# Last layer of a four-layer pair network: the order of TensorE's products and transposes, the way the totals are made, and the place of the residual copies

## The reference, cut to what matters

```python
x = x + _L3_conv_ref(_gn(x), L3_conv_Ws, L3_conv_Wm, L3_conv_bm)

# in _L3_conv_ref(X, Ws, Wm, bm), with L(v, i) = v @ Ws[i - 1]:
ret = L(X, 10) + L(X.transpose(0, 2, 1, 3), 11)
ret = ret + (L(sum_of_rows, 6) + L(sum_of_cols, 8) + L(diag_part, 12))[:, :, None, :]
ret = ret + (L(sum_of_rows, 7) + L(sum_of_cols, 9) + L(diag_part, 13))[:, None, :, :]
ret = ret + 2.0 * L(sum_diag_part, 14)[:, None, None, :]
diag_term = L(diag_part, 1) + L(sum_of_rows, 3) + L(sum_of_cols, 4) + (L(sum_diag_part, 2) + L(sum_all, 5))[:, None, :]
ret = ret + diag_term[:, :, None, :] * eye[None, :, :, None]
return jax.nn.relu(ret @ Wm + bm)
```

## Time and profile before

| | before |
|---|---|
| median of 3 runs | 1118.38 us (1118.35 to 1118.80) |
| the profiled execution | 1116.33 us, of which its span (first to last instruction) is 1114.5 us |
| busy over the span | PE 1029.5 us (92%), DVE 743.7, ACT 519.3, POOL 410.6 |
| granted TensorE clock, mean | 0.958 of full |
| last norm block, from the barrier to the next one | 1062.9 to 1066.9 us |
| block of `layer3` | 1066.9 to 1114.5 us, 47.6 us |
| PE busy in one pair of its steps | 3.11 of 4.40 us |

### The profile page before, as it was taken

How to read it: one execution, slowest core, us unless ns; L and a number is a source line. 1 busy time by engine, 2 the same in 40 slices (tenths; PEclk the granted TensorE clock), 3 DMA queues, 4 the chain that set the end, 5 groups by cost and what they waited for, 6 DMA issues and landing times. The chain is left out here.

```text
span 1114.5 us, 24968 instructions
## 1 busy us (share of the span) xinstructions
PE 1029.5 (92%) x9092; PEld 736.1 (66%) x9092; DVE 743.7 (67%) x3631; ACT 519.3 (47%) x1133; POOL 410.6 (37%) x555
## 2 busy tenths in 40 slices
PE   5887999999999699779999999999999999999966
PEld 4435888888887343357777777777777777777632
DVE  3685888888887323456767777676777667676353
ACT  2485777777777100124343443434344343434344
POOL 0154666666666200011332323233232333323245
PEclk8899999999999699859999999999999999999969
DMA  8000000000000000000000000000000000000033
GB/s 174 2 0 2 3 2 3 3 3 2 3 2 3 1 1 1 10 1 1 1 2 1 2 1 2 1 1 1 1 1 2 1 1 1 2 1 1 1 86 141
DMA packets 14045, 13.01 MB, mean 12 GB/s; under 512 B 3300, under 2 KB 11748, under 8 KB 13924
## 3 DMA queue, kind: packets, MB, share of 16 engines
q1 hardware_dynamic: 12548, 10.84, 3.9%
q10 hardware_dynamic: 1376, 0.59, 0.3%
HBM read 5.14 MB, written 4.19 MB: 8 GB/s over the span
## 5 line engine op out<-in xcount | busy, mean ns | idle before, releaser
L1606 PE MATMUL quad<-theta,nat 128*128 128x512 f32 x512 | 240.8, 593 | 0.0
L730 POOL TENSOR_TENSOR nat<-nat,arena 128x512 f32<-128x512 f32 x128 | 131.7, 1050 | 39.4 <-DVE arena L788 35.6
L1614 PEld LDWEIGHTS quad<-flat 128*128 128x128 f32 x768 | 104.3, 190 | 46.9 <-ACT flat L1400 24.1
L1606 PEld LDWEIGHTS quad<-theta,nat 128*128 128x128 f32 x512 | 87.5, 191 | 61.7 <-issue 61.7
L1614 PE MATMUL quad<-flat 128*128 128x128 f32 x768 | 124.7, 285 | 2.1 <-ACT flat L1400 1.0
L788 DVE CUSTOM_DVE_ANT_0 nat<-quad,arena 128x128 f32<-128x128 f32 x512 | 111.2, 282 | 1.4 <-PE quad L874 1.4
L1400 ACT ACTIVATE flat<-quad 128x256 f32<-128x256 f32 x192 | 73.5, 383 | 74.5 <-PE quad L1614 57.9
L747 ACT ACTIVATE nat<-bank 128x512 f32<-128x512 f32 x128 | 73.1, 598 | 65.3 <-PE bank L882 65.3
L1357 POOL COPY img<-flat 64x256 f32<-64x256 f32 x63 | 25.1, 399 | 186.2 <-DVE nat L1515 171.7
L882 PE MATMUL bank<-const,nat 128*128 128x128 f32 x512 | 73.3, 276 | 8.8 <-ACT nat L747 8.0
L752 ACT ACTIVATE nat<-nat 128x512 f32<-128x512 f32 x128 | 77.2, 634 | 3.8 <-POOL nat L730 3.8
(11 more groups left out here) (386 smaller groups left out, 2313.2 us busy)
## 6 DMA issues: line engine op xcount, KB each, us to landing
out<-nat SPq DMA_DIRECT2D x16, 256.0 KB, 2.0
flat<-img SPq DMA_DIRECT2D x2, 640.0 KB, 8.5
flat<-img SPq DMA_DIRECT2D x1, 512.0 KB, 4.9
const<-in_constants ACTq DMA_DIRECT2D x1, 400.5 KB, 3.2
flat<-img SPq DMA_DIRECT2D x1, 256.0 KB, 3.3
arena<-in_L_conv_Ws SPq DMA_DIRECT2D x1, 240.0 KB
nat<-in_x SPq DMA_DIRECT2D x4, 0.2 KB, 12.1
arena<-in_L_conv_Wq ACTq DMA_DIRECT2D x1, 32.0 KB, 7.0
```

Source lines behind the costliest of these rows:

```text
L730: pool.tensor_tensor(scored, scored, of_head(least[b], h).broadcast_to([128, ROWS, L]), ALU.subtract).then_inc(lowered, 1)
L1606: return pe.matmul(m.quad[:, n, :], vT[:, col(n)], m.theta[:, part, :], start=(part == 0), stop=False, skip_group_check=True)
L1614: last = pe.matmul(m.quad[:, row, place * C:(place + 2) * C], a8[g % 2][:, col(row)], zs[half][k % 2][:, n, :], start=False, stop=(k == 2) ...
```

## The change

Five edits, all in the last layer:

- On PE the two products of later steps stand ahead of the two transposes in each turn of the loop, where they stood behind them.
- Each total is made for both halves of the partitions: each weight is multiplied twice, once into each half, and the column and diagonal totals take only the 64 columns of that half (every second one, `own`). The constants are added by PE in the same accumulation, as products with a vector repeated over 64 columns (`level`).
- DVE copies the finished totals: one copy for `of_row` and one for `of_col` instead of six instructions, two for `diag_pair` instead of four.
- Five of the sixteen residual copies of ACT stand in the norm block, ahead of the square root.
- The other eleven stand ahead of the first Relu; none is among the steps any more.

```diff
@@ group_norm
+            if act_aside is not None:
+                act_aside(act)
             act.wait_ge(S("group_var"), layer + 1)
@@ layer3
-    totals, diag_totals = B[0], B[1]
+    row_totals, col_totals, diag_totals = B[0][:, 0:L], B[0][:, L:L + L // 2], B[1][:, 0:L // 2]
+    EARLY = 5
+    def first_copies(act):
+        for t in range(EARLY):
+            copy_half(act, t)
-    group_norm(nc, m, 3, pool_aside=sums_of_cols, dve_aside=raw_rows)
+    group_norm(nc, m, 3, pool_aside=sums_of_cols, dve_aside=raw_rows, act_aside=first_copies)
@@ DVE
             dve.wait_ge(terms_made, 1)
-            for q in range(2):
-                step(dve.tensor_copy(level[halves[q], 0:1], totals[halves[0], 2 * L:2 * L + 1]))
-                dve.tensor_scalar(of_col[halves[q], :], totals[halves[0], L + q:2 * L:2], level[halves[q], 0:1], None, ALU.add)
-                step(dve.tensor_copy(of_row[halves[q], :], totals[halves[0], 0:L]))
+            dve.tensor_copy(of_row, row_totals)
+            step(dve.tensor_copy(of_col, col_totals))
...
                 for q in range(2):
-                    step(dve.tensor_copy(level[halves[q], 1:2], diag_totals[halves[0], L:L + 1]))
-                    last = dve.tensor_scalar(diag_pair[halves[q], :, q], diag_totals[halves[0], q:L:2], level[halves[q], 1:2], None, ALU.add)
+                    last = dve.tensor_copy(diag_pair[halves[q], :, q], diag_totals[halves[q], :])
@@ ACT
-            AHEAD = 10
-            for t in range(AHEAD):
-                copy_half(t)
+            for t in range(EARLY, STEPS3):
+                copy_half(act, t)
...
-                if t + AHEAD < STEPS3:
-                    copy_half(t + AHEAD)
@@ PE
+            def total(into, vectors, first=True, done=True):
+                for n, (weights, vector_of) in enumerate(vectors):
+                    for q in range(2):
+                        last = pe.matmul(into[halves[q], :], weights, vector_of(q), start=(first and n == 0),
+                                         stop=(done and n == len(vectors) - 1), skip_group_check=True)
+                return last
...
+            def own(vector):
+                return lambda q: vector[:, q:L:2]
+            def level(vector):
+                return lambda q: vector.broadcast_to([vector.shape[0], L // 2])
...
             for t in range(0, STEPS3, 2):
-                turn(t)
-                turn(t + 1)
                 for later in (t + 4, t + 5):
                     if later < STEPS3:
                         mixed(later)
+                turn(t)
+                turn(t + 1)
```

More of the change, by code:

```diff
@@ L394, in _, with group_norm @@
             turn_banks(at_bank, BANKS)
-def group_norm(nc, m, layer, loads=(), loaded=None, pool_aside=None, dve_aside=None):
+def group_norm(nc, m, layer, loads=(), loaded=None, pool_aside=None, dve_aside=None, act_aside=None):
     rows = 128
@@ L1776, in layer3 @@
     col_half = m.take(L)
-    of_row, of_col, level = m.take(L), m.take(L // 2), m.take(2)
+    of_row, of_col = m.take(L), m.take(L // 2)
     diag_pair = m.take(L).rearrange("p (s q) -> p s q", q=2)
@@ L1816, in raw_rows, with copy_half @@
         dve.tensor_copy(diag_raw, m.img[0:C, 0:L * L:L + 1])
-    group_norm(nc, m, 3, pool_aside=sums_of_cols, dve_aside=raw_rows)
+    EARLY = 5
+    def copy_half(act, t):
+        act.activation(*residual_half(0, t, t + 1), ACT.Copy).then_inc(m.sem("copied"), 1)
+    def first_copies(act):
+        for t in range(EARLY):
+            copy_half(act, t)
+    group_norm(nc, m, 3, pool_aside=sums_of_cols, dve_aside=raw_rows, act_aside=first_copies)
     prepared, terms_made = S("prepared"), S("terms_made")
@@ L1908, in _, with whole @@
         def _(pe):
-            def total(bank, place, vectors):
-                for n, (weights, vector) in enumerate(vectors):
-                    last = pe.matmul(bank[halves[0], place], weights, vector, start=(n == 0), stop=(n == len(vectors) - 1))
-                return last
+            def total(into, vectors, first=True, done=True):
[3 more added lines that the diff above has]
+                                         stop=(done and n == len(vectors) - 1), skip_group_check=True)
+                return last
+            def whole(vector):
+                return lambda q: vector
+            def own(vector):
+                return lambda q: vector[:, q:L:2]
+            def level(vector):
+                return lambda q: vector.broadcast_to([vector.shape[0], L // 2])
             def mixed(t):
@@ L1937, in _ @@
             pe.wait_ge(prepared, 2)
-            total(totals, column(1), [(kind(7), rows_x), (kind(9), cols_x), (kind(13), diag_x)])
-            total(totals, column(0), [(kind(6), rows_x), (kind(8), cols_x), (kind(12), diag_x)])
+            total(row_totals, [(kind(6), whole(rows_x)), (kind(8), whole(cols_x)), (kind(12), whole(diag_x))])
+            total(col_totals, [(kind(7), own(rows_x)), (kind(9), own(cols_x)), (kind(13), own(diag_x))], done=False)
             pe.wait_ge(prepared, 3)
-            total(totals, slice(2 * L, 2 * L + 1), [(kind(14), mean[:, 2:3]), (both_kinds, shift), (bm, m.one[:, 0:1])]).then_inc(terms_made, 1)
+            total(col_totals, [(kind(14), level(mean[:, 2:3])), (both_kinds, level(shift)), (bm, level(m.one[:, 0:1]))],
+                  first=False).then_inc(terms_made, 1)
             mixed(1)
-            total(diag_totals, column(0), [(kind(1), diag_x), (kind(3), rows_x), (kind(4), cols_x)])
-            total(diag_totals, slice(L, L + 1), [(kind(2), mean[:, 1:2]), (kind(5), mean[:, 0:1])]).then_inc(terms_made, 1)
+            total(diag_totals, [(kind(1), own(diag_x)), (kind(3), own(rows_x)), (kind(4), own(cols_x)),
+                                (kind(2), level(mean[:, 1:2])), (kind(5), level(mean[:, 0:1]))]).then_inc(terms_made, 1)
             for t in range(2, 4):
```

2 lines of the change are left out of this document (removed).

## The result

The kernel after takes 1108.57 us, the median of four runs (1107.96 to 1113.64); the kernel before took 1118.37 beside it (1117.38 to 1118.8). The ratio is 0.9924, 95% interval 0.9904 to 0.9944, so 8.5 us less (6.3 to 10.7); the medians lie 9.8 apart. The prediction said 1108.1 in 1106.9 to 1110.2.

A forecast was written before the change was run, and what follows sets the result against it. It took a ring of waits to bound the last layer's steps and PE its start; products 6 4.36 us earlier plus 5.92 over four pairs made 10.3 off the median 1118.38, so 1108.1 us, range 1106.9 to 1110.2.

The forecast's parts named there:

- The ring: Last layer's steps: DVE waits for PE, POOL for DVE, PE for POOL; a pair of steps takes 4.40 us, no engine full.
- The pair: Two steps of the loop: PE's own distances sum to 2.92 us (2.88 to 3.03), POOL just below at 2.78.
- The totals: Block's start on PE: passes run in twos; first totals 2.75 us, second 1.17, each 0.62 less; products 2 start 1.24 earlier.
- DVE's copies: Behind the second totals: two copies take about 0.5 us instead of 0.97; fewer behind the first totals are worth nothing.
- ACT's copies: Five in the norm end 0.3 us ahead of the square root, eleven ahead of the first Relu; worth nothing, cost nothing.
- The sum: Last layer: products 6 come 4.36 us earlier, four pairs save 5.92, so products 14 come 10.3 earlier.
- the steps had 1.00: Against the slower rival: clock stays at half through the steps, 5.45 us a pair, 1121.5 us; chance 0.03.
- the totals ran in twos: Against the rival of totals running singly at the block's start: products 6 only 2.5 us earlier, 1110.0 us; chance 0.10.
- ACT closed no ring: Against the rival that ACT's Relu behind a later copy-out closes a ring: 3.5 us per pair, 1110.4 us; chance 0.06.
- the order did what it says: Against the rival that an unseen wait holds the products: only the start's 1.2 to 1.7 us left, 1116.9; chance 0.02.
- The rival of an earlier clock: Block's start: denser totals raise the clock earlier, products 2 to 5 at full clock, POOL binds; 1107.0 us; chance 0.11.
- a later rise: Products 4 and 5 and transposes 0 and 1 all at half clock: products 6 only 2.6 us earlier, 1109.9; chance 0.08.

The follow-up runs named there:

- the order alone: Kernel before with only PE's products of steps t+4 and t+5 put ahead of the transposes of t and t+1: 1108.78 us beside 1119.23, ratio 0.9903.
- the three halved kernels: Kernel after with half of each step's transposes, half of the residual's addition, or both left out: 1108.2, 1108.75, 1110.62 us; pairs 2.67, 2.89, 2.45.
- both runs: ACT's residual copies alone moved in the kernel before: 1119.01 us, ratio 0.9996; moved back to their old places in the kernel after: 1109.74, ratio 0.9911.
- half the transposes: Kernel after with two of the four transposes of each step left out: 1108.2 us, one run; block end 35.91 us behind product 0 instead of 37.00.
- the kernel kept at work: Kernel after with six matmuls added on PE around the last norm, results unread: 1105.28 us beside 1120.07, ratio 0.9867.
- the copies alone: Kernel before with only ACT's residual copies moved, five into the norm, eleven ahead of the steps: 1119.01 us beside 1119.23, ratio 0.9996.

## Why the prediction was right, point by point

**The ring.** It was named as the bound of the steps, with the order on PE as its cause, and the order alone takes it away: pair 4.40 to 2.89, 9.98 us at the end, 9.63 at POOL's last diagonal.

**The pair.** 0.58 + 1.87 + 0.47 = 2.92 was forecast. Measured after: from transposes to products 1092.74 - 1091.71 = 1.03 for both groups; from products to transposes 1091.71 - 1089.85 = 1.86. Sum 2.89. The second group starts at 1092.21, so the distance that no row of before showed is 0.49 and not 0.47, and the one to the products 0.53 and not the 0.58 that was read where PE had waited; together they bring the sum 0.03 below the forecast. That PE would set it, with POOL just below, is borne out by the three halved kernels.

**The totals.** That passes come in twos and that a two of 64 columns costs n = 0.112, was right: the 28 passes from 1071.07 to 1073.26 are 6 twos of 128 and 8 of 64 columns, (2.19 - 6 x 0.216) / 8 = 0.112. The Trainium skill (TensorEngine Tiling (Array Packing), Instruction Overhead) says that a matmul with one column has the same latency as one with 60. The distances of starts agree here: a two of 64 columns takes what a single pass of one column took, 0.112. The mis-sized term is the gaps: the two twos on `shift` take 0.36 and the two on `one` 0.40 (1073.26 to 1073.62 to 1074.02), where 4 x 0.112 stood. So the first totals took 2.95 instead of 2.75 and the second 1.26 instead of 1.17, and products 2 came 0.95 earlier instead of 1.24.

**DVE's copies.** The two behind the second totals took 0.46, about 0.5 was said; POOL's diagonal of step 1 followed 1.21 behind DVE's start of it (1077.80 to 1079.01), as taken from the pair.

**ACT's copies.** Five end at 1067.56, 0.34 ahead of the square root, which stands 3.03 behind the norm's start as before; eleven end at 1074.94, ahead of the first Relu at 1078.16. Worth nothing, shown by both runs.

**The sum.** Products 6 were to be 4.36 earlier and are 4.23: the totals lacked 0.29, and since the clock rises at its own time, what this pushes behind the rise takes half as long there, some 0.15. Four pairs at 2.89 instead of 2.92 give 0.12 back. Products 14 are 10.27 earlier, 10.3 was said: misses of 0.13 and 0.12 that cancel. From products 14 to the end it is 10.54 after and 10.55 before, the same work as was said. The median then came out 0.5 above the forecast; that it came so close is in part luck, as the runs of the kernel after lie 5.7 us apart. One figure in the prediction doesn't agree with itself: it puts POOL some 0.8 us ahead of PE at diagonal 14, while its own times for that, 1094.9 and 1096.0, are 1.1 apart. With half the transposes, where POOL sets the steps, diagonal 14 came 0.81 earlier than after (27.98 against 28.79 behind product 0).

**What the sum didn't say** is how little the totals' own edit adds. By its steps they seemed to bring over a microsecond of the 10.3; beside the order they bring 0.62 at POOL's last diagonal and 0.30 at the end, since what the order alone left was POOL's lateness, and that was small. The sum was right because PE's path with both edits was followed, not because its parts add up.

**The rivals.** The clock rose 12.62 behind product 0, neither earlier nor later than before, and the steps had 1.00; the totals ran in twos; ACT closed no ring; the order did what it says. The rival of an earlier clock was right in its mechanism, POOL bound from its first step, as the kernel kept at work shows; it was asked of denser totals, and these didn't bring it.

**The clock.** The sum takes the rise at 1079.84 of the profile before as fixed to product 0, and the prediction holds an earlier and a later rise as rivals. In the ten profiles without the added products it came 12.57 to 12.75 behind product 0 in eight, but 10.86 with half the transposes and 14.24 with the copies alone, where PE's work up to then was that of other kernels in the table. So it doesn't hang on PE's work since product 0 alone, and what else sets it stays open. That it came where the sum had it, 12.62 against 12.59, was likely and not sure: a rise 1.9 earlier was worth 0.94 at products 6.

## What to carry to other kernels

Where no engine is full and the waits form a ring, look for the instruction that stands in a queue behind a wait that it doesn't need: putting it in front was worth 10 us here, and every other part of the change under 2. Price an edit at what the next bound leaves of it, with the other edits in place: at POOL's last diagonal the totals were worth 1.4 alone, 0.6 behind the order, and 1.3 again once PE was fast enough to leave the end to POOL. And follow the clock into the gap ahead of a stage: a few products that nobody reads and that fill it were worth more than all that was done to the totals.

## What the runs showed that was not expected

- Filling PE's gap in the norm kept the clock at 1.00 and took 4.68 us off a 37 us block. The norm didn't lose by it: its square root came 2.59 behind the norm's start instead of 3.03, because its own small products took 0.38 instead of 0.59.
- In the kernel after, PE was busy 9.83 of 10.20 us and the clock stayed at 0.50 for all of it. The Trainium skill (TensorE: Matmul & The Clock Gate, Part 1) says that activity lifts the clock. Here the clock rose 12.62 us behind product 0, and not sooner with the denser totals.
- Passes for the two halves of the partitions overlap even where six of one half stand ahead of six of the other: 25 passes in 2.32 us, against some 2.0 in twos and 4.0 singly.
- Stretches of passes that end in a change of kind are longer than their columns say: the totals on `shift` by 0.36 - 0.22 = 0.14 us, those on `one` by 0.18, products ahead of transposes by 1.86 - 4 x 0.43 = 0.14, transposes ahead of products by about as much (1.03 against 8 x 0.43 / 4 = 0.86). Two such changes are 0.3 of each pair's 2.89; no run tried a loop with fewer.
